# Newton's step and the bonus products on GpSimd, squares on ScalarE, and the group norm's centring inside the merge

## The reference, cut to what matters

```
def step(s, rkvw):                       # s: 8 x 8 for each of 32 heads
    a = k_t[..., :, None] * v_t[..., None, :]
    out = einsum('bhi,bhij->bhj', r_t, u * a + s)
    s = a + w_t[..., :, None] * s
...
og = out.reshape(b, l, h, 8)
m = og.mean(-1); va = ((og - m) ** 2).mean(-1)
og = ((og - m) / sqrt(va + 1e-05)).reshape(b, l, e) * gn_w + gn_b
x1 = x + og * g @ Wo.T
...
kk = square(relu(xk2 @ Wfk.T))           # the channel mixing
x  = x1 + sigmoid(xr2 @ Wfr.T) * (kk @ Wfv.T)
```

## Time and profile before

| | |
|---|---|
| median of three runs | 1918.36 us |
| the profiled execution | 1919.72 us |
| its span | 1917.9 us |
| mean granted clock of TensorE | 0.986 |
| busy: TensorE, VectorE, ScalarE, GpSimd | 96%, 58%, 55%, 52% |

### The profile page before, as it was taken

How to read it: one execution, slowest core, us unless ns; L and a number is a source line. 1 busy time by engine, 2 the same in 40 slices (tenths; PEclk the granted TensorE clock), 3 DMA queues, 4 the chain that set the end, 5 groups by cost and what they waited for, 6 DMA issues and landing times.

```text
span 1917.9 us, 37676 instructions
## 1 busy us (share of the span) xinstructions
PE 1843.9 (96%) x14304; PEld 1498.2 (78%) x14304; DVE 1113.1 (58%) x2100; ACT 1045.6 (55%) x1949; POOL 1000.1 (52%) x1140
## 2 busy tenths in 40 slices
PE   7999999989986999999999999999999999999999
PEld 5777789534454778888888888888888888967798
DVE  4666665489989555454444444445444547756574
ACT  4566553434344656665656656556566565346542
POOL 6777741376654544654544545445445445347530
PEclk9999999989998999999999999999999999999999
DMA  6000010000001222322332333223223310010000
GB/s 242 2 2 2 2 58 1 1 1 1 1 1 50 76 74 91 98 83 83 101 94 83 89 95 94 83 84 110 83 84 94 98 52 23 23 45 2 2 12 34
DMA packets 61841, 108.01 MB, mean 56 GB/s; under 512 B 7008, under 2 KB 42336, under 8 KB 60256
## 3 DMA queue, kind: packets, MB, share of 16 engines
q1 hardware_dynamic: 60784, 103.38, 17.1%
q10 hardware_dynamic: 880, 2.22, 0.3%
HBM read 103.47 MB, written 2.10 MB: 55 GB/s over the span
## 4 chain that ended last, share of the span: by engine, by line
PE 86%; DVE 7%; issue 3%; ACT 2%; POOL 2%; DMA 0%; DVEq 0%; SPq 0%; ACTq 0%; POOLq 0%
PE banks L866 18%; PE banks L937 9%; PE banks L894 9%; PE banks L471 7%; PE banks L629 7%; PE banks L646 7%; PE banks L926 6%; PE banks L907 3%; PE banks L480 3%; PE banks L553 3%; PE banks L539 2%; PE banks L528 2%; PE banks L510 2%; PE banks L465 2%; DVE banks L1690 1%
## 5 line engine op out<-in xcount | busy, mean ns | idle before, releaser
L2026 POOL TENSOR_TENSOR w_lo<-w2ring,w_hi 128x512 fp32r<-128x512 f32 x128 | 180.0, 1406 | 245.0 <-ACT w_hi L1150 245.0
L1843 DVE TENSOR_REDUCE nmax<-banks 128x4 f32<-128x260 f32 x128 | 54.1, 423 | 308.5 <-PE banks L907 308.5
L2109 POOL TENSOR_TENSOR wo_lo<-wo_ring,wo_hi 128x256 fp32r<-128x256 f32 x128 | 93.7, 742 | 238.6 <-ACT wo_hi L1358 238.5
L1831 DVE TENSOR_TENSOR v<-banks,dbv 128x512 f32<-128x512 f32 x128 | 88.5, 691 | 157.6 <-PE banks L894 157.5
L1358 ACT ACTIVATE wo_hi<-wo_ring 128x256 fp32r<-128x256 f32 x128 | 53.0, 417 | 186.2 <-PE banks L937 185.3
L937 PE MATMUL banks<-wo_hi,c_hi 128*128 128x256 f32 x512 | 147.1, 287 | 0.8 <-DVE c_lo L1836 0.8
L937 PE MATMUL banks<-wo_lo,c_hi 128*128 128x256 f32 x512 | 144.7, 283 | 0.0
L937 PE MATMUL banks<-wo_hi,c_lo 128*128 128x256 f32 x512 | 144.6, 282 | 0.0
L1345 ACT ACTIVATE k<-banks,cols 128x512 f32<-128x512 f32 x128 | 88.2, 689 | 80.4 <-PE banks L866 80.4
L926 PE MATMUL banks<-PT,v 128*128 128x128 f32 x1024 | 124.7, 275 | 1.0 <-issue 0.8
L926 PEld LDWEIGHTS banks<-PT,v 128*128 128x128 f32 x1024 | 119.8, 192 | 1.7 <-issue 1.2
(11 more groups left out here) (236 smaller groups left out, 5418.0 us busy)
## 6 DMA issues: line engine op xcount, KB each, us to landing
w2ring<-in_w SPq DMA_DIRECT2D x128, 384.0 KB, 3.2
b2ring<-in_b SPq DMA_DIRECT2D x128, 128.0 KB, 4.0
wo_ring<-in_wo SPq DMA_DIRECT2D x128, 128.0 KB, 3.1
mlp_w<-in_mlp SPq DMA_DIRECT2D x6, 1024.0 KB, 7.5
wl<-in_wres SPq DMA_DIRECT2D x1, 2688.0 KB, 8.7
X<-in_x_in SPq DMA_DIRECT2D x4, 512.0 KB, 11.5
wb<-in_wres SPq DMA_DIRECT2D x2, 1024.0 KB, 10.8
ctxT<-in_ctx_in SPq DMA_DIRECT2D x4, 512.0 KB, 18.8
```

The source lines that it names most:

```text
L1831: V.tensor_tensor(v2[i], held(("v2", v, i)).rearrange("p (s d) -> p s d", s=HV), dbv, ALU.add).then_inc(S["l2_v"], 1)
L2026: G.tensor_tensor(w2_lo[:, n % 2, :], w2ring[:, n % HR, 0:2 * KT * P], w2_hi[:, n % 2, :].bitcast(f32), ALU.subtract).then_inc(S["l2_wlo"], 1)
L2109: G.tensor_tensor(wo_lo[:, n % 2, :], wo_ring[:, n % WR, :], wo_hi[:, n % 2, :].bitcast(f32), ALU.subtract).then_inc(S["l2_wolo"], 1)
```

## The change

- The merge multiplies with constant matrices that subtract the group's mean in the same product (`center_f` of 128 columns, `center_s` of 2 x 256 columns), brought by one DMA to the place of three bias rows that are no longer used; ScalarE copies the result out of the bank. The products with `oS` stream 256 columns where they streamed 128. Half h = 0 is merged in step 3 and half 1 in step 5.
- For chunks 0 to 2, Newton's step is done by GpSimd (`sharpen`, step 10), and VectorE multiplies both halves in step 11. Chunk 3's stays on VectorE.
- The bonus products are GpSimd's (`bonus_weights`, step 15).
- The mixing's squares are ScalarE's, right behind the relu. The mixing's output for chunk 0 moves from step 5 to 7 and its addition from 7 to 8.
- In `attention`, the split comes in step p = 2 of the last chunk instead of after the loop. In the first MLP, `before(0, 0)` and `before(0, 1)` are done at n = 29 and 30.
- At the end of the recurrence the orders on ScalarE, VectorE and GpSimd change as shown; the addition of the cross attention's bias for its first chunk moves behind the first four heads' weights.

The diff, with indentation taken off and most unchanged lines left out:

```
@@ -38,6 +38,7 @@
 FIRST_PIECES = 2
+FIRST_STEP = CHUNKS * MT - 1 - FIRST_PIECES
 HV = 4
...
@@ -165,6 +166,9 @@
 rows = view(keep("rows", len(ROWS) * D), "p (r d) -> p r d", d=D)
+
+center = at("center", held_to[0] - len(ROWS) * D, P + 2 * D)
+center_f, center_s = center[:, 0:P], view(center[:, P:], "p (q n) -> p q n", q=2)
 consts_at = held_to[0]
...
@@ -343,7 +346,7 @@
     sem, ("vectors_in", "w_qkv_in", "w_self_in", "w_cross_in", "w_l1_in", "w_l3_in", "preset", "masks_in", "rows_in", "state_in"))
-s_ident, s_rows0, s_sel = sem("ident_in"), sem("first_rows_in"), sem("select_in")
+s_ident, s_rows0, s_sel, s_center = sem("ident_in"), sem("first_rows_in"), sem("select_in"), sem("center_in")
 s_x = [sem(f"x_in{c}") for c in range(CHUNKS)]
...
@@ -687,22 +690,22 @@
-def tokens_first(c):
-
+def tokens_first(c, h):
+
+    if c + h == 0:
+        pe.wait_ge(s_center, 16)
     pe.wait_ge(S["l1_oS"], 2 * (c + 1))
     pe.wait_ge(S["l1_uv"], KT * (c + 1))
-    for h in range(2):
-        b = take(pe, ("og", c, h), "l1_cent", 2 * c + h + 1, MIDDLE)
-        for i in range(2):
-            tok = slice((2 * h + i) * P, (2 * h + i + 1) * P)
-            out = b[:, i * D:(i + 1) * D]
-            for k in range(KT):
-                mm(out[:, k * P:(k + 1) * P], rku[c % 2][:, k, tok], ident, start=(i + k == 0), stop=False,
-                   skip_group_check=True)
-            for q in range(2):
-                last = mm(out.rearrange("p (x q j) -> p q j x", q=2, j=4)[:, q], oS[:, q, tok], ident,
-                          start=False, stop=(i + q == 2), skip_group_check=True)
-        last.then_inc(S["l1_og"], 1)
+    b = take(pe, ("og", c, h), "l1_cent", 2 * c + h + 1, MIDDLE)
+    for i in range(2):
+        tok = slice((2 * h + i) * P, (2 * h + i + 1) * P)
+        out = b[:, i * D:(i + 1) * D]
+        for k in range(KT):
+            mm(out[:, k * P:(k + 1) * P], rku[c % 2][:, k, tok], center_f, start=(i + k == 0), stop=False,
+               skip_group_check=True)
+        for q in range(2):
+            last = mm(out, oS[:, q, tok], center_s[:, q], start=False, stop=(i + q == 2), skip_group_check=True)
+    last.then_inc(S["l1_og"], 1)
@@ -725,8 +728,7 @@
 n = 4 * KT * c + KT * (i - 1) + k
-used_by = ("l1_rku", KT * c + k + 1) if f == 3 else ("l1_rkvg", n + 1)
-linear(("rkvg", n), l1w[:, {3: 0, 0: 1, 2: 2, 4: 3}[f]], x, k * P, "l1_rkvg_mm", *used_by, among=MIDDLE)
+linear(("rkvg", n), l1w[:, {3: 0, 0: 1, 2: 2, 4: 3}[f]], x, k * P, "l1_rkvg_mm", "l1_rkvg", n + 1, among=MIDDLE)
@@ -758,8 +760,8 @@
     total(QUADS * c + QUADS - 1)
-if j == 3:
-    tokens_first(c)
+if j in (3, 5):
+    tokens_first(c, j // 2 - 1)
 if j == 12:
@@ -844,7 +846,7 @@
     mixing_in(j // 8, 1)
-if j in (5, 13):
+if j in (7, 13):
     mixing_out(j // 8)
@@ -853,6 +855,7 @@
 after(CHUNKS - 1, 3)
+after(CHUNKS - 1, 5)
 fronts(EARLY)
@@ -1224,11 +1227,17 @@
 if j in (5, 7):
-    h = (j - 5) // 2
+    h = j // 2 - 2
     act.wait_ge(S["l1_cent"], 2 * c + h + 1)
...
     A(norm_tiles(c)[0], gn[:, h, :], ACT.Square).then_inc(S["l1_sq"], 1)
+if j in (4, 6):
+    h = j // 2 - 2
+    act.wait_ge(S["l1_og"], 2 * c + h + 1)
+    if c:
+        act.wait_ge(S["l1_gn_tp"], KT * c)
+    A(gn[:, h, :], held(("og", c, h)), ACT.Copy).then_inc(S["l1_cent"], 1)
 if j == 9:
@@ -1244,6 +1253,10 @@
     A(mixing_tiles(c)[2][:, k, :], held(("ffk", c, k))[:, :], ACT.Relu).then_inc(S["l1_relu"], 1)
+
+for k in range(KT):
+    act.wait_ge(S["l1_relu"], KT * c + k + 1)
+    A(mixing_tiles(c)[3][:, k, :], mixing_tiles(c)[2][:, k, :], ACT.Square).then_inc(S["l1_kk"], 1)
@@ -1302,14 +1315,16 @@
 after(last, 2)
+after(last, 4)
+after(last, 5)
 normed(EARLY)
-after(last, 5)
+after(last, 6)
+weights_hi(0)
 fronts(EARLY)
-act.wait_ge(S["l1_og"], 2 * CHUNKS)
+after(last, 7)
+weights_hi(1)
 for n in range(2):
-    weights_hi(n)
     value_weights_hi(n)
-after(last, 7)
 after(last, 9)
@@ -1586,11 +1601,12 @@
             values(ai, g)
+    if p == 2 and ai + 1 == stop:
+        split(it + 1)
     if p == 3 and ai + 1 < stop:
...
 n = UNITS * stop - 1
-split(attended(stop - 1) + 1)
 largest(n)
@@ -1622,8 +1638,8 @@
     split(it + 1)
-if m == 0 and n >= CHUNKS * MT - FIRST_PIECES:
-    before(0, n - CHUNKS * MT + FIRST_PIECES)
+if m == 0 and n - FIRST_STEP in range(FIRST_PIECES):
+    before(0, n - FIRST_STEP)
 yield 1
@@ -1668,11 +1684,6 @@
                                ALU.add, ALU.mult).then_inc(S["l1_y"], 1)
-if j == 14:
-    for k in range(KT):
-        n = 4 * KT * c + 2 * KT + k
-        dve.wait_ge(S["l1_rkvg"], n + 1)
-        V.tensor_tensor(rku[c % 2][:, k, :], held(("rkvg", n)), kuT[:, k, :], ALU.mult).then_inc(S["l1_rku"], 1)
@@ -1698,30 +1709,31 @@
     squares, var, sd, root = norm_tiles(c)
-    if piece == 0:
-        dve.wait_ge(S["l1_og"], 2 * c + h + 1)
-        if c:
-            dve.wait_ge(S["l1_gn_tp"], KT * c)
-        og = held(("og", c, h)).rearrange("p (g j) -> p g j", j=S8)
-        settle(V.tensor_reduce(gn_sum[:, h, :], og, AX, ALU.add))
-        V.scalar_tensor_tensor(xg, gn_sum[:, h, :].unsqueeze(2).to_broadcast([P, 64, S8]), -1.0 / S8,
-                               og, ALU.mult, ALU.add).then_inc(S["l1_cent"], 1)
     if piece == 1:
...
     if piece == 2:
-        if h == 0:
-            dve.wait_ge(S["l1_sd"], c + 1)
+        if c == CHUNKS - 1 and h == 0:
+            dve.wait_ge(S["l1_rec"], CHUNKS)
             total, sd, r = flat(var), flat(sd), flat(root)
-            settle(V.reciprocal(r, sd))
             settle(V.scalar_tensor_tensor(sd, r, -0.5 / S8, r, ALU.mult, ALU.mult))
...
             settle(V.scalar_tensor_tensor(r, sd, 1.5, r, ALU.add, ALU.mult))
+        if c < CHUNKS - 1:
+            dve.wait_ge(S["l1_root"], c + 1)
+        dve.wait_ge(S["l1_cent"], 2 * c + h + 1)
         V.tensor_tensor(xg, xg, root[:, h, :].unsqueeze(2).to_broadcast([P, 64, S8]), ALU.mult).then_inc(S["l1_gn"], 1)
...
 def after(c, j):
-    if j in (4, 5, 6, 8, 10, 11):
-        group_norm(c, *{4: (0, 0), 5: (1, 0), 6: (0, 1), 8: (1, 1), 10: (0, 2), 11: (1, 2)}[j])
+    if j in (6, 8):
+        group_norm(c, j // 2 - 3, 1)
+    if j == 10:
+        sd, root = norm_tiles(c)[2:]
+        dve.wait_ge(S["l1_sd"], c + 1)
+        V.reciprocal(flat(root), flat(sd)).then_inc(S["l1_rec"], 1)
+    if j == 11:
+        for h in range(2):
+            group_norm(c, h, 2)
     if j == 13:
@@ -1749,21 +1761,12 @@
-def squared(c):
-    raised, squares = mixing_tiles(c)[2:4]
-
-    dve.wait_ge(S["l1_ffk_mm"], KT * (c + 1))
-    for k in range(KT):
-        dve.wait_ge(S["l1_relu"], KT * c + k + 1)
-        V.tensor_tensor(squares[:, k, :], raised[:, k, :], raised[:, k, :], ALU.mult).then_inc(S["l1_kk"], 1)
-
 def late(p):
...
         after(last, 11)
-        squared(2)
     if p == 1:
@@ -1773,7 +1776,6 @@
 if p == 4:
-    squared(3)
     stats(CHUNKS * L2A + 1)
@@ -1803,21 +1805,17 @@
             mixed(j // 8)
-        if j in (3, 12):
-            squared(j // 8)
-        if j in (7, 14):
-            update(CHUNKS * FFN + j // 8)
+        if j in (8, 14):
+            update(CHUNKS * FFN + j // 12)
         if j == 8:
...
 split(CHUNKS * L2A)
-after(last, 4)
-after(last, 5)
 after(last, 6)
+after(last, 8)
 mixed(2)
-after(last, 8)
 yield None
@@ -2056,6 +2054,23 @@
+def sharpen(c):
+
+    total, sd, r = (flat(x) for x in norm_tiles(c)[1:])
+    pool.wait_ge(S["l1_rec"], c + 1)
+    settle(G.tensor_tensor(sd, r, r, ALU.mult))
+    settle(G.tensor_scalar(total, total, -0.5 / S8, -0.5 * EPS, ALU.mult, ALU.add))
+    settle(G.tensor_tensor(sd, sd, total, ALU.mult))
+    settle(G.tensor_scalar(sd, sd, 1.5, 0.0, ALU.add, ALU.add))
+    G.tensor_tensor(r, r, sd, ALU.mult).then_inc(S["l1_root"], 1)
+
+def bonus_weights(c):
+    for k in range(KT):
+        pool.wait_ge(S["l1_rkvg"], 4 * KT * c + 2 * KT + k + 1)
+        if c >= 2:
+            pool.wait_ge(S["l1_og"], 2 * (c - 1))
+        G.tensor_tensor(rku[c % 2][:, k, :], r1T[c % 2][:, k, :], kuT[:, k, :], ALU.mult).then_inc(S["l1_rku"], 1)
+
 def weigh(n):
@@ -2075,6 +2090,8 @@
             G.memset(sequences(flat(tile[p]).bitcast(f32))[:, :, 0], x).then_inc(S["slots_zero"], 1)
+if j == 15:
+    bonus_weights(0)
 yield 1
@@ -2084,7 +2101,11 @@
     before(c + 1, j)
-else:
+    if j == 15:
+        bonus_weights(c + 1)
+if c and j == 10:
+    sharpen(c - 1)
+if c + 1 == CHUNKS:
     if j in (1, 9):
@@ -2096,11 +2117,11 @@
 context_parts_lo(0)
+weights_lo(0)
+weights_lo(1)
 mixing_shift(2)
 for n in range(2):
-    weights_lo(n)
     value_weights_lo(n)
-bias(CHUNKS * L2A)
 yield None
@@ -2131,6 +2152,7 @@
     value_weights_lo(n + 2)
+bias(CHUNKS * L2A)
 for n in range(0, NH, 2):
@@ -2228,6 +2250,7 @@
 load_weights(sp, s_wl1, wl1, "L1_m1", "L1_W")
+sp.dma_start(center, t_center).then_inc(s_center, 16)
 sp.wait_ge(S["l1_rs_used"], CHUNKS * QUADS)
@@ -2271,6 +2294,16 @@
     return np.concatenate([parts[n].astype(np.float32) for n, _ in CONSTS], axis=1)
+
+
+def centering():
+
+    p, f = np.arange(P), np.arange(D)
```

(6 more changed lines are left out.)

6 lines of the change are left out of this document (2 added, 4 removed).

## The result

The changed kernel takes 1907.13 us (median of five runs, 1905.77 to 1908.44); the kernel before, run beside it, 1917.98 (five runs, 1915.57 to 1918.41). The ratio is 0.9943, 95% interval 0.9931 to 0.9954: 10.85 us faster, where I forecast 14.4 less and 1904.0. So the two traces differ by 13.9 us in span, of which some 3 are the choice of executions.

What follows compares the result with a forecast made beforehand. TensorE was taken to bound most of the kernel, VectorE mattering only in the recurrence; -7.2 - 2.0 - 3.0 - 1.0 - 1.2 = -14.4 us from the profiled 1919.72 gave 1905.3, or 1904.0 for the median, range 1894 to 1912.

Steps and rivals of the forecast that it cites:

- likeliest case: Whole kernel: the summed forecast holds, recurrence mostly held by TensorE and ScalarE; 1899 to 1909 us, chance 0.47.
- the third rival: Recurrence gives nothing, TensorE's extra work and new waits eat the freed time; hand-overs alone give 9.2, 1909 us, chance 0.23.
- Attention to MLP: Two ends of attention: the split in step p = 2 gains 3.5 to 3.6 us each, 7.2 in all.
- MLP to recurrence: First MLP's end: two pieces one step earlier remove TensorE's wait of 1.97 us, gaining 2.0, passed on whole.
- The recurrence: Recurrence: 1.5 us gained in each of periods 1 and 2, 0 in period 0, 1 in period 3.
- the term for Newton's step: Recurrence, steps 10 and 11: GpSimd takes 2.3 us, VectorE waits 0.5, multiplies in 1.3; 1.6 us gained.
- the bound of 2.4: Recurrence, periods 1 and 2: TensorE's gaps of 4.1 us less 1.7 more work allow at most 2.4 us gain each.
- The bonus products: Recurrence: on GpSimd they are ready at 545.5, TensorE reads them at 547.11, a slack of 1.6 us.
- ScalarE, period 3: Recurrence, period 3: squares on ScalarE delay step 4's first state by 1.2 us; of some 8 us freed, 1 is gained.
- Recurrence to cross attention: Start of cross attention: low parts before the mixing's shift, TensorE starts at 621.3 instead of 622.54, gaining 1.2 us.
- The fifth rival: Slower: GpSimd becomes the recurrence's bound, adding 17 us there; about 13 us slower in all, 1931, chance 0.08.
- the signs named ahead: Changed profile: no low-input waits at hand-overs, periods 1 and 2 about 55 us; wrong if under 54 or over 57.

Runs made afterwards that it cites:

- the experiment: The changed kernel with the attention split and the earlier first two pieces in the first MLP taken back: 1917.87 us, ratio 0.9994.
- the best kernel: The changed kernel with Newton's step and bonus products back on VectorE and GpSimd reordered behind the recurrence: 1897.65 us, ratio 0.9887.

## Why the prediction was right, and where it was not

- **Direction and likeliest case.** The time lies within the range, 3.1 us above the forecast. The case forecast as likeliest (its own range 1899 to 1909) holds 1907.1, but in outcome the third rival, "the recurrence gives nothing", is nearer at 1909: the hand-overs gave 9.9 of 10.85 us, where I had them at 9.2 of 14.4. What that rival said of the reason was half right: the freed time was eaten on GpSimd and, for lack of it, on VectorE; ScalarE's copies and squares ate none.
- **Attention to MLP, forecast 7.2.** Measured 3.96 + 3.86 = 7.8. The split took 4.26 us again and step p = 3 came late as forecast: its reciprocal is at 229.05 instead of 229.73, 0.7 earlier where all before it was 1.6 earlier, so 0.9 late (1.1 forecast). But the size is right partly by luck, for my 3.5 held no clock. In each of the two places up to 1.7 us of full speed were lost behind the wait of 3.12 and are not now (last section); by this reckoning, an estimate, the order alone gave about 2.2 in each.
- **MLP to recurrence, forecast 2.0.** Measured 2.2, no wait left. It is passed on whole.
- **The recurrence, forecast 4.0.** Measured 1.2 in the traces, 0.7 by the medians of the experiment. This is the step that failed, and in it the term for Newton's step. (A further 1.0 us of the difference to 4.0 is period 0, which I had at 0 and which the low clock made longer; without it the traces show 2.2.) I let GpSimd end at 525.5, VectorE wait 0.5 and multiply in 1.3, and took 1.6 us as gained. It waits 1.20 and multiplies in 2.34, and steps 10 and 11 are 0.33 longer than before instead of shorter. GpSimd's duration was hardly the error (2.6 us, 2.3 forecast); I had priced VectorE's multiplications at a figure of undisturbed ones, although had shown me 4.25 for 1.36 beside GpSimd. With the step on VectorE, periods 1 and 2 of the best kernel are 2.1 and 2.0 shorter than before; the bound of 2.4 that TensorE's gaps set was sound.
- **The bonus products, forecast free.** TensorE had them in time: no wait for them in any period, with 0.8 us to spare in period 1 (ready at 426.4, read at 427.25) where I had 1.6. They cost 1.7 us at another place, on VectorE in steps 0 and 1 of period 1, by the same collision. In period 2 they cost nothing: VectorE's steps 0 and 1 take 6.99, before 6.98. There it was before the change that the small part of the shift met GpSimd (489.78, 1.25 us), and it cost nothing either; now it takes 0.18 and VectorE waits 0.78 for the first state instead.
- **ScalarE, period 3, forecast 1 us gained.** It gained 2.5. The late first state was there (step 3 takes 6.09 instead of 4.35), but in the main through the clock in the product ahead of the squares, and it was given back in the next three steps; the squares taken off VectorE in step 12 gave 2.3. I had counted a delay on ScalarE as lost without asking what stood behind the step that it delayed.
- **Recurrence to cross attention, forecast 1.2 gained.** The first product came 1.7 earlier, counted from the last step, yet the mixing product 1.9 later. I had followed GpSimd's queue to the first two heads only. Two low parts of the value weights (2.41 us), the key's bias, four small operations for the values' bias and a clearing of 0.95 us stand before the low parts of heads 2 and 3. They stood there before too, but then the mixing's shift (1.7 us) was over when the first product began; now it is still to come, and TensorE meets the queue.
- **The fifth rival**, GpSimd as bound of the recurrence, had the right mechanism at a seventh of its price: 1.7 once and 0.3 twice, 2.4 us where it had 17. (In period 3 steps 10 and 11 are 1.7 longer too, 8.88 for 7.18, but the period is no shorter in the best kernel, 60.70, which has them at 8.21.)

Of the signs named ahead: period 2 at 55.9, between the bounds of 54 and 57, and no wait for the low input at the hand-overs came true; period 1 at 57.4 is over the 57 that I had said would prove me wrong, and proves it for the bonus products.

## What to carry to other kernels

An operation moved from VectorE to GpSimd costs the time by which both engines' operations lengthen where they meet, so it has to be laid beside the neighbour's row with both at their long durations; here three small operations of 0.3 us were cheaper left alone. A piece of work that is made to start earlier meets the next queue, so follow that queue to the second and third thing that it delivers. And the waits of 3 us of TensorE at the hand-overs cost more than 3 us each, so the two short edits there were worth nearly all of the gain; in the busy stage what some edits gained others took back. Last, lay the clock's stretches over two traces before you put a difference of 1 or 2 us in a stage down to an edit.
